# The order of GpSimd's two large multiplies in a selective-scan block on one core

## The chip, the cores and the metric

One core of one Trainium2 chip runs the whole block: layer norm, a selective scan (the Mamba kind) with a gate, a residual, a second layer norm and a top-2 mixture of low-rank experts. The metric is the device time of the core in microseconds (us), as the median of three runs. Two names recur: DVE is VectorE, POOL is GpSimd, and ACT, PE and SP are ScalarE, TensorE and SyncE.

## The reference, cut to what matters

The input is 4 sequences of 2048 tokens with 256 features. The change lies in the scan:

```
u_inner = u @ W_in.T + b_in;  x, z = split(u_inner)          # 512 channels each
dbc = x @ W_x.T + b_x                                        # 16 for delta, 16 for B, 16 for C
delta = softplus(dbc[:16] @ W_dt.T + b_dt);  A = -exp(A_log)  # A: 512 x 16
h = h * exp(delta * A) + (delta * x) * B                     # state, 512 x 16 per token
y = sum over the 16 states of h * C
y = (y + x * D) * silu(z);  out = y @ W_out.T + b_out
```

A feed-forward part with expert routing follows; it is computed by the same engines in between.

## The kernel before, in words

The tokens are worked in 16 chunks of 512. A chunk's scan has 512 channels times 16 states, that is 8192 rows, laid on 128 partitions as 64 units; it is done in 16 **steps** of 4 units each. Step `s` has `m = s // 4` (a block of 128 channels) and `k = s % 4` (four of the states). I write scan(s,j) for unit j of step s, and number the steps of the next chunk from 0 again, with a prime where it matters. For each step:

- POOL does the **B multiply**, B(s): one instruction on 128 x 2048 elements, `hs[s % 4] = dx_rep[m % 2] * b_rep[k]` (`times_b`, line 1051). It waits for the sum of step s-4, whose `hs` buffer it takes over, and at k = 0 for the DMA that brings `dx_rep` (line 446). It signals `input_ready`.
- ACT computes the decay factors `exp(dt * A)` into PSUM, 4 instructions (line 785).
- DVE runs four scans, 128 x 512 each (line 964). scan(s,0) waits for `input_ready` of step s. Each starts from `state`, the last column of the same unit in the chunk before, and the scan of the last chunk is kept by ACT, two units at a time (`keep_state`, line 799).
- The **C product** multiplies the scanned states by C. DVE does units 0 and 1 (line 954), right after scan(s,2). Units 2 and 3 are POOL's in the steps with s % 3 != 0, ten of sixteen (line 1063, `times_c`, which I write C(s)), and DVE's in the other six, after scan(s+1,0). POOL's C(s) waits for all four scans of step s (`scan_done`) and for ACT's copy of their last columns (`state_kept`), because it writes over `hs`. It signals `prod_pool`.
- PE sums over the states into `y_ps` with four matmuls (line 651), two steps behind the scan.

Each engine runs its own program in order, and between the steps stand side jobs, placed by hand in tables (`PE_SIDE`, `ACT_SIDE`, `DVE_SIDE`, `POOL_SIDE`): projections of the next chunk ("pre"), the gate ("main"), output projection and routing of the last one ("post"), the experts ("late"). ACT copies the last columns of units 2 and 3 of step s-1 in its own step s, behind two decay instructions of step s and the side jobs placed at its units 0 and 1.

POOL's step s is B(s+1), then C(s-1) where that one is POOL's, then the side jobs of that row of `POOL_SIDE`. The side jobs are: step 0: A1; 1: O1; 2: S3, G2, G3; 3: V1; 4: U1; 5: A2; 6: S0; 7: O2, G0; 9: S1; 10: G1, S2; 11: V0; 12: U0; 13: W0. S and G (lines 1004 and 1008) are 128 x 512, V and U (lines 1041 and 1001) 128 x 1024, and the others are chains of tiny instructions. R is a job of the last chunk alone. G waits for a Y job of DVE (line 865), the reading of `y_ps`. U produces `z_dt`, which SP stores to DRAM and loads back, spread over the partitions, as `dx_rep`: U0 for the next chunk's m = 0, so that B(0') waits for that way round, and U1 for m = 2, used by B(8).

SP's queue loads `b_rep` and `c_rep` for the next chunk: `b_rep[k]` waits for `input_ready` of the steps 12 + k, `c_rep[k]` for the products of the same steps, POOL's among them. POOL issues no DMA.

Of the kernel before, what the change touches and what calls it, by code (L numbers as in the profile page):

```python
# [36 lines left out]
STEPS = M * KG  # L37
# [202 lines left out]
def block_program(nc, u, w_in, b_in, w_x, b_x, w_dt, b_dt, a_log, d_skip, w_out, b_out, w_ga, b_g, w_i, w_o,  # L240
                  lora_b, ident_in, nsum_in, tri_in, out):
    with ExitStack() as ctx:
# [168 lines left out]
        def side(engine, s, j, parts):  # L411

            for job in SIDE[engine][s][j]:
                if job.split()[1] in parts:
                    yield job[0], int(job[1]), job.split()[1], job
# [577 lines left out]
        def _(pool):  # L993
# [49 lines left out]
            def times_b(c, par, s):  # L1043

                m, k = divmod(s, KG)
                if k == 0:
                    pool.wait_ge(rep_loaded[m % 2], 256 * c + 128 * (m // 2 + 1))
                if m == 0:
                    pool.wait_ge(b_loaded[k], 64 * (c + 1))
                at_least(pool, nsum_done, STEPS * c + s - 3)  # L1050
                nc.gpsimd.tensor_tensor(hs[s % 4][:], dx_rep[m % 2][:], b_rep[:, k, :].unsqueeze(1).to_broadcast([P, J, T]),  # L1051
                                        ALU.mult).then_inc(input_ready, 1)

            def times_c(c, s):

                if s not in POOL_STEPS:
                    return
                k = s % KG
                pool.wait_ge(scan_done, UNITS * c + J * (s + 1))
                pool.wait_ge(state_kept, 2 * (STEPS * c + s + 1))  # L1060
                if s < KG:
                    pool.wait_ge(c_loaded[k], 64 * (c + 1))
                nc.gpsimd.tensor_tensor(hs[s % 4][:, 2:4, :], hs[s % 4][:, 2:4, :],  # L1063
                                        c_rep[:, k, :].unsqueeze(1).to_broadcast([P, 2, T]), ALU.mult).then_inc(prod_pool, 1)

            def body(c, par, parts):
                for s in range(STEPS):
                    if "main" in parts:
                        if s + 1 < STEPS:
                            times_b(c, par, s + 1)  # L1070
                        elif "pre" in parts:
                            times_b(c + 1, par, 0)
                        if s >= 1:
                            times_c(c, s - 1)
                    if s == 0 and "post" in parts:
                        times_c(c - 1, STEPS - 1)
                    for job in side("pool", s, 0, parts):
                        job_pool(*job, c, par)
                if "main" not in parts and "pre" in parts:
                    times_b(0, par, 0)  # L1080

            sweep(pool, body)


# [53 lines left out]
```

## Time and profile before

| | |
|---|---|
| median of 3 runs | 2150.73 us (2149.88 to 2154.53) |
| the profiled execution: its own time | 2150.39 us |
| its span | 2148.6 us |
| POOL busy | 1885.0 us (88%) x892 |
| DVE busy | 1861.7 us (87%) x2256 |
| PE busy | 1693.7 us (79%) x7648 |
| ACT busy | 1422.8 us (66%) x2756 |

The times are read so: the span runs from the first to the last instruction, and the time of a run has some 2 us around it. Busy shares are averages over the start, sixteen chunks and a tail of some 115 us in which the last chunk's experts are computed. What matters for the steps is a chunk in the middle, so the rows further below are taken from there. "POOL hs L1051" is the B multiply, "POOL hs L1063" POOL's C product, "DVE decay L964" a scan. A start-to-start distance is a little shorter than the duration printed, since an engine starts an instruction while the one before writes its last results.

### The profile page before, as it was taken

What the parts mean: (1) busy time and instruction counts of PE and PEld (TensorE: products, weight loads), DVE (VectorE), ACT (ScalarE), POOL (GpSimd) and SP (SyncE); (2) the same over time, 40 slices, a digit from 0 to 9 for tenths busy, and PEclk for the clock granted to TensorE, in tenths of its full rate; (3) what the DMA queues carried; (4) which work ended last, traced back from release to release, by engine and by line L of the source; (5) the groups of instructions that cost most, each with busy time, mean ns of one, the idle gap of its engine ahead of it and who ended that gap; (6) DMA issues with size and microseconds to landing.
All of it is one profiled execution on the core that took longest, in us unless ns stands there. A gap on an engine that the chain in (4) does not pass through costs nothing.

```text
span 2148.6 us, 28539 instructions
## 1 busy us (share of the span) xinstructions
PE 1693.7 (79%) x7648; PEld 939.9 (44%) x7648; DVE 1861.7 (87%) x2256; ACT 1422.8 (66%) x2756; POOL 1885.0 (88%) x892
## 2 busy tenths in 40 slices
PE   3253669888887978888797978879798888877898
PEld 1011225444544545454454544444454445444474
DVE  1698989999998989999898998999899999989810
ACT  2565657767676766777676776867677676766522
POOL 1799999999999999999998998999999998999701
PEclk8575879999998999999999999999999999999998
DMA  3645443553545355354644444454535535453100
GB/s 137 142 106 142 109 118 91 129 128 85 133 102 152 82 128 130 88 120 105 160 98 119 111 104 126 100 145 105 133 91 129 127 83 126 102 150 86 35 8 13
DMA packets 145762, 235.19 MB, mean 109 GB/s; under 512 B 21040, under 2 KB 45872, under 8 KB 145072
## 3 DMA queue, kind: packets, MB, share of 16 engines
q1 hardware_dynamic: 145584, 233.18, 43.4%
q8 instruction: 67, 1.10, 0.2%
q14 instruction: 111, 0.91, 0.1%
HBM read 190.11 MB, written 42.99 MB: 108 GB/s over the span
## 4 chain that ended last, share of the span: by engine, by line
PE 29%; POOL 27%; issue 18%; DVE 10%; DMA 8%; SPq 4%; ACT 3%; POOLq 0%; DVEq 0%; ACTq 0%
POOL hs L1051 14%; POOL hs L1063 6%; PE bank L586 6%; PE y_ps L651 4%; DVE decay L964 4%; PE bank L632 4%; PE bank L600 4%; PE bank L637 4%; PE bank L619 4%; DMA b_rep<-bc_scratch 4%; DVE hs L954 3%; DMA rep_scratch<-z_dt 2%; SPq L446 2%; POOL e_dt L1041 2%; DVE hs L964 2%
## 5 line engine op out<-in xcount | busy, mean ns | idle before, releaser
L1051 POOL TENSOR_TENSOR hs<-dx_rep,b_rep 128x2048 f32<-128x2048 f32 x256 | 1161.7, 4539 | 101.0 <-DMA dx_rep<-rep_scratch 100.4
L964 DVE TENSOR_TENSOR_SCAN decay<-decay,state,hs 128x512 f32<-128x512 f32 x704 | 881.0, 1275 | 98.1 <-POOL hs L1051 86.4
L785 ACT ACTIVATE decay<-dt_rep,a_sb 128x512 f32<-128x512 f32 x1024 | 677.4, 684 | 28.0 <-DMA dx_rep<-rep_scratch 10.7
L651 PE MATMUL y_ps<-hs,nsum 128*32 128x512 f32 x2048 | 298.4, 658 | 207.2 <-POOL hs L1063 96.4
L954 DVE TENSOR_TENSOR hs<-decay,c_rep 128x1024 f32<-128x1024 f32 x352 | 422.9, 1201 | 0.0
L964 DVE TENSOR_TENSOR_SCAN hs<-decay,state,hs 128x512 f32<-128x512 f32 x320 | 406.0, 1269 | 2.2 <-ACT decay L785 1.6
L1063 POOL TENSOR_TENSOR hs<-hs,c_rep 128x1024 f32<-128x1024 f32 x160 | 378.3, 2364 | 4.3 <-ACT state L799 3.7
L632 PE MATMUL bank<-ident,r 128*128 128x128 f32 x1920 | 284.4, 309 | 69.8 <-ACT r L763 30.8
L632 PEld LDWEIGHTS bank<-ident,r 128*128 128x128 f32 x1920 | 260.9, 218 | 135.6 <-ACT r L763 35.1
L619 PE MATMUL bank<-w_i_sb,x_t 128*128 128x512 f32 x512 | 259.9, 631 | 56.9 <-ACT e_dt L706 15.8
L799 ACT COPY state<-decay 128x2 f32<-128x2 f32 x352 | 56.6, 161 | 334.3 <-DVE hs L954 323.2
L586 PE MATMUL bank<-xn_t,w_in_sb 128*128 128x512 f32 x512 | 253.4, 625 | 23.3 <-ACT r L763 15.1
L637 PE MATMUL bank<-w_o_sb,r_t 128*128 128x256 f32 x1024 | 238.8, 387 | 2.2 <-ACT e_gate L725 1.6
L637 PEld LDWEIGHTS bank<-w_o_sb,r_t 128*128 128x128 f32 x1024 | 192.1, 192 | 44.5 <-issue 16.6
L651 PEld LDWEIGHTS y_ps<-hs,nsum 128*32 128x32 f32 x2048 | 43.1, 111 | 317.2 <-issue 220.1
L619 PEld LDWEIGHTS bank<-w_i_sb,x_t 128*128 128x128 f32 x512 | 90.9, 194 | 169.4 <-issue 89.2
L586 PEld LDWEIGHTS bank<-xn_t,w_in_sb 128*128 128x128 f32 x512 | 93.1, 199 | 139.8 <-issue 98.7
L759 ACT ACTIVATE r<-bank,wgt 128x512 f32<-128x512 f32 x128 | 86.4, 675 | 76.5 <-PE bank L620 63.8
L600 PE MATMUL bank<-w_out_sb,gated 128*128 128x256 f32 x512 | 121.8, 382 | 1.7 <-DVE x L873 1.2
L600 PEld LDWEIGHTS bank<-w_out_sb,gated 128*128 128x128 f32 x512 | 94.7, 190 | 34.2 <-DVE x L873 13.9
L770 ACT COPY r_t<-bank 128x512 f32<-128x512 f32 x128 | 73.4, 573 | 42.2 <-PE bank L637 31.7
L763 ACT ACTIVATE r<-bank,wgt 128x512 f32<-128x512 f32 x128 | 86.2, 674 | 19.3 <-PE bank L562 18.4
(99 smaller groups left out, 1731.8 us busy)
## 6 DMA issues: line engine op xcount, KB each, us to landing
dt_rep<-rep_scratch SPq DMA_DIRECT2D x256, 256.0 KB, 4.4
dx_rep<-rep_scratch SPq DMA_DIRECT2D x256, 256.0 KB, 7.3
b_rep<-bc_scratch SPq DMA_DIRECT2D x256, 64.0 KB, 2.9
rep_scratch<-e_dt SPq DMA_DIRECT2D x32, 512.0 KB, 2.8
rep_scratch<-z_dt SPq DMA_DIRECT2D x32, 512.0 KB, 3.7
c_rep<-bc_scratch SPq DMA_DIRECT2D x256, 64.0 KB, 2.1
xin<-in_u SPq DMA_DIRECT2D x16, 512.0 KB, 3.6
xr<-in_u SPq DMA_DIRECT2D x16, 512.0 KB, 3.8
```

Of the source, the lines that this page charges most:

```text
L586: mm = pe.matmul(ps[:], w_in_sb[:, k, col:col + P], xn_t[odd][:, k, :], start=k == 0, stop=k == KD - 1)
L600: pe.matmul(ps[:, 0:D], gated[odd][:, k, i * P:(i + 1) * P], w_out_sb[:, k, :], start=k == 0, stop=False)
L619: pe.matmul(ps[:], x2_t[odd][:, k, t * P:(t + 1) * P], w_i_sb[:, k, cols], start=k == 0, stop=False)
L632: mm = pe.matmul(ps[:, f * P:(f + 1) * P], r[i % 2][:, f * P:(f + 1) * P], ident[:], start=r is r1, stop=r is r2)
L637: mm = pe.matmul(ps[:, 0:D], r_t[:, f, :], w_o_sb[:, f, :], start=f == 0, stop=f == NF - 1)
L651: mm = pe.matmul(y_ps[32 * j:32 * j + 32, :], nsum[:], hs[s % 4][:, j, :], start=k == 0, stop=k == KG - 1)
L759: nc.scalar.activation(r1[i % 2][:], ps[:], ACT.Relu, scale=wgt[odd][:, 0, i // 2:i // 2 + 1]).then_inc(r1_ready, 1)
L785: nc.scalar.activation(decay[:, j, :], dt_rep[m % 2][:, j, :], ACT.Exp, scale=a_sb[:, J * s + j:J * s + j + 1]).then_inc(decay_ready, 1)
L954: v.tensor_tensor(hs[s % 4][:, js, :], decay[:, js, :], c_rep[:, k, :].unsqueeze(1).to_broadcast([P, 2, T]), ALU.mult).then_inc(prod_vecto ...
L964: v.tensor_tensor_scan(hs[s % 4][:, j, :] if kept else decay[:, j, :], decay[:, j, :], hs[s % 4][:, j, :], state[:, b, n:n + 1], ALU.mult, ...
L1051: nc.gpsimd.tensor_tensor(hs[s % 4][:], dx_rep[m % 2][:], b_rep[:, k, :].unsqueeze(1).to_broadcast([P, J, T]), ALU.mult).then_inc(input_re ...
L1063: nc.gpsimd.tensor_tensor(hs[s % 4][:, 2:4, :], hs[s % 4][:, 2:4, :], c_rep[:, k, :].unsqueeze(1).to_broadcast([P, 2, T]), ALU.mult).then_ ...
```

## The change

In GpSimd's program the order inside a step becomes C(s-1), B(s+1), side jobs. The jobs, their waits and their number stay. The product of step 15, which stands at step 0 of the next chunk, moves with the others in the text; since 15 % 3 = 0 it is not POOL's and is no instruction.

```diff
             def body(c, par, parts):
                 for s in range(STEPS):
+                    if s == 0 and "post" in parts:
+                        times_c(c - 1, STEPS - 1)
                     if "main" in parts:
+                        if s >= 1:
+                            times_c(c, s - 1)
                         if s + 1 < STEPS:
                             times_b(c, par, s + 1)
                         elif "pre" in parts:
                             times_b(c + 1, par, 0)
-                        if s >= 1:
-                            times_c(c, s - 1)
-                    if s == 0 and "post" in parts:
-                        times_c(c - 1, STEPS - 1)
                     for job in side("pool", s, 0, parts):
                         job_pool(*job, c, par)
```

## Rows read from the trace of the kernel before

**Rows 1.** Busy us of PE, PEld, DVE, ACT, POOL: first chunk, one in the middle

```profile
67.30:182.10 114.80, 51.22 (x164) 15.16 (x164) 105.40 (x100) 70.86 (x136) 109.27 (x42) 0.65 0.51 120
1044.98:1168.20 123.22, 103.20 (x485) 58.52 (x484) 115.84 (x141) 88.43 (x173) 117.21 (x55) 0.97 0.47 116
```

**Rows 2.** Groups of POOL's instructions by shape: busy, mean ns, idle before

```profile
L1051 POOL TENSOR_TENSOR hs<-dx_rep,b_rep 128x2048 f32<-128x2048 f32 x256 | 1161.7, 4539 | 101.0 <-DMA dx_rep<-rep_scratch 100.4 <-PE y_ps L651 0.5
L1063 POOL TENSOR_TENSOR hs<-hs,c_rep 128x1024 f32<-128x1024 f32 x160 | 378.3, 2364 | 4.3 <-ACT state L799 3.7 <-issue 0.5
L1004 POOL TENSOR_TENSOR z_gate<-z_gate,e_gate 128x512 f32<-128x512 f32 x64 | 82.0, 1282 | 0.0
```

**Rows 3.** POOL in order of time, from step 13 to step 0 of the next chunk

```profile
1028.65 4.55 POOL L1051 TENSOR_TENSOR hs<-dx_rep,b_rep 128x2048 f32<-128x2048 f32 x1
...
1033.31 4.53 POOL L1051 TENSOR_TENSOR hs<-dx_rep,b_rep 128x2048 f32<-128x2048 f32 x1
1037.79 2.37 POOL L1063 TENSOR_TENSOR hs<-hs,c_rep 128x1024 f32<-128x1024 f32 x1
1044.98 4.52 POOL L1051 TENSOR_TENSOR hs<-dx_rep,b_rep 128x2048 f32<-128x2048 f32 x1 [4.83 <-DMA dx_rep<-rep_scratch]
1049.45 2.35 POOL L1063 TENSOR_TENSOR hs<-hs,c_rep 128x1024 f32<-128x1024 f32 x1
1051.76 4.54 POOL L1051 TENSOR_TENSOR hs<-dx_rep,b_rep 128x2048 f32<-128x2048 f32 x1
```

**Rows 4.** What DVE waited for over the whole span: us, times, longest

```profile
DVE decay L964 <- POOL hs L1051: 86.4, 47, 25.2
DVE gated L865 <- PE y_ps L651: 41.8, 30, 3.5
```

**Rows 5.** DVE in order of time: scan(0,0)

```profile
1049.62 1.29 DVE L964 TENSOR_TENSOR_SCAN decay<-decay,state,hs 128x512 f32<-128x512 f32 x1 [3.18 <-POOL hs L1051]
```

**Rows 6.** DVE busy in steps 0 and 1, 4 and 5, 7, 10, 13

```profile
1049.62:1065.66 16.04, 15.65 (x21) 0.89 0.75 180
1078.37:1096.36 17.99, 17.17 (x26) 1.00 0.30 96
1102.20:1109.83 7.63, 7.63 (x9) 1.00 0.19 38
1123.32:1131.56 8.24, 8.24 (x8) 1.00 0.81 170
1147.42:1157.24 9.82, 7.82 (x8) 0.83 0.29 107
```

**Rows 7.** DVE in order of time: scan(s,3) of steps 1, 5, 7, 10, 13

```profile
1064.47 1.28 DVE L964 TENSOR_TENSOR_SCAN hs<-decay,state,hs 128x512 f32<-128x512 f32 x1
...
1093.67 1.25 DVE L964 TENSOR_TENSOR_SCAN hs<-decay,state,hs 128x512 f32<-128x512 f32 x1
...
1108.64 1.27 DVE L964 TENSOR_TENSOR_SCAN hs<-decay,state,hs 128x512 f32<-128x512 f32 x1
...
1130.37 1.27 DVE L964 TENSOR_TENSOR_SCAN hs<-decay,state,hs 128x512 f32<-128x512 f32 x1
...
1156.05 1.27 DVE L964 TENSOR_TENSOR_SCAN hs<-decay,state,hs 128x512 f32<-128x512 f32 x1
```

**Rows 8.** ACT in order of time: the copies of those steps' last columns

```profile
1066.02 0.18 ACT L799 COPY state<-hs 128x2 f32<-128x2 f32 x1
...
1096.68 0.17 ACT L799 COPY state<-hs 128x2 f32<-128x2 f32 x1
...
1112.12 0.19 ACT L799 COPY state<-hs 128x2 f32<-128x2 f32 x1
...
1132.87 0.18 ACT L799 COPY state<-hs 128x2 f32<-128x2 f32 x1
...
1158.64 0.20 ACT L799 COPY state<-hs 128x2 f32<-128x2 f32 x1
```

**Rows 9.** SP's queue in order of time: the last reload of b_rep

```profile
1051.15 1.69 SPq L453 DMA_DIRECT2D b_rep<-bc_scratch  x4
```

## The prediction

> **What bounds the kernel now.** I read the busy time of single chunks first. A chunk in the middle takes 123.22 us, and in it POOL is busy 117.21 us and DVE 115.84 us [rows 1]: two engines are full, and neither has as much as 8 us to spare. The groups of POOL's instructions show what the rest is: before B multiplies POOL idles 101.0 us in the whole run, nearly all for the DMA that brings dx_rep, and before its C products only 4.3 us [rows 2]. POOL in order of time shows the place: once a chunk, before B(0), it stands 4.83 us [rows 3]. DVE's waits are small too: 86.4 us for B multiplies, 25.2 us of it once, at the start, and 41.8 us for the sum that its Y jobs read [rows 4]. So POOL sets the pace, DVE runs just behind it, and what keeps both full is slack between them: POOL can multiply B(s+1) while DVE is still in step s-1, and asks for scan(s-1,3) only after it.
>
> **The change.** No instruction is added or removed. C(s-1), which needs DVE to have finished step s-1, now stands ahead of B(s+1), which DVE needs for step s+1. B(s+1) so gets DVE's progress as a condition that it did not have. Behind a waiting C(s-1) are queued B(s+1), on which DVE waits, and the side jobs of the step. After scan(s-1,3) POOL needs a C and a B, 6.8 us, before DVE may start step s+1, and DVE has only its step s to do meanwhile. Where step s is shorter than that, DVE stalls; where POOL is early, it stalls; and what one loses is no longer made up by the other.
>
> **The terms.** Start to start a B takes 1037.79 - 1033.31 = 4.48 us and a C 1051.76 - 1049.45 = 2.31 us [rows 3]; V and U have the C's shape, 2.31 us. A 128x512 side job prints 1.28 us [rows 2], less the 0.05 us by which 4.54 and 4.48 differ: 1.23 us. From the end of a B to the scan that it releases is 1049.62 - (1044.98 + 4.52) = 0.12 us [rows 3, 5]; I take 0.12 us for the release of a C by ACT's copy too. DVE's stretches run from the start of scan(s,0), which is where each window of [rows 6] begins, to the end of scan(s,3) [rows 7]: steps 0 and 1, 1065.75 - 1049.62 less 0.39 us idle (16.04 - 15.65) = 15.74 us; steps 4 and 5, 1094.92 - 1078.37 = 16.55 us; step 7, 7.71 us; step 10, 8.32 us; step 13, 9.90 us less the 2.00 us that Y2 idles (9.82 - 7.82), which go, since C(11) comes a B multiply sooner: 7.90 us. From scan(s,3)'s end to the end of ACT's copy [rows 7, 8]: step 1, 0.45 us; 5, 1.93; 7, 2.40; 10, 1.41; 13, 1.52. These lags are mostly side jobs that ACT's program puts ahead of the copy (two behind step 7, one long one behind step 10, two behind step 13), so they stay. Behind step 5 the program puts none, and there I take step 1's 0.45 us and keep 1.93 for the range.
>
> **One chunk of the new kernel**, from the end of B(0) to the end of the next chunk's B(0), following whoever is waited for:
> 1. DVE, steps 0 and 1, while POOL does B(1), A1, B(2), O1 (under 11 us) and then waits for C(1)'s data: 0.12 + 15.74 + 0.45 + 0.12 = 16.43 us.
> 2. POOL: C(1), B(3), S3, G2, G3, C(2), B(4): 2 x 6.79 + 3 x 1.23 = 17.27 us. DVE waits for B(3) and B(4).
> 3. DVE, steps 4 and 5: 0.12 + 16.55 + 0.45 + 0.12 = 17.24 us, against POOL's V1, B(5), U1, C(4), B(6), A2 (16.4 us).
> 4. POOL: C(5), B(7): 6.79 us.
> 5. DVE, step 7: 0.12 + 7.71 + 2.40 + 0.12 = 10.35 us, against POOL's S0, B(8), O2, G0 (8.3 us).
> 6. POOL: C(7), B(9), C(8), B(10): 13.58 us. DVE waits for both B.
> 7. DVE, step 10: 0.12 + 8.32 + 1.41 + 0.12 = 9.97 us, against POOL's 8.2 us.
> 8. POOL: C(10), B(12), V0, C(11), B(13): 2 x 6.79 + 2.31 = 15.89 us.
> 9. DVE, step 13: 0.12 + 7.90 + 1.52 + 0.12 = 9.66 us, against POOL's 7 us.
> 10. POOL: C(13), B(15), C(14), B(0): 13.58 us.
>
> The sum is 130.76 us, 7.54 us more than 123.22. POOL waits about 5.6, 0.8, 2.0, 1.8 and 2.7 us in parts 1, 3, 5, 7 and 9, some 13 us in place of its 5.2 at the DMA. That DMA no longer shows: before, B(0) starts 1044.98 - 1028.65 = 16.33 us after U0 [rows 3], now part 9's rest (7.35), 6.79 and 2.31 lie between, 16.4 us. It is just behind the new wait, and takes over if that shrinks.
>
> **What costs nothing.** PE gets POOL's product one B sooner and its sums earlier; they are off the pace. SP: the reload of c_rep comes sooner; that of b_rep waits for B multiplies that come up to 2.31 us later in their step, yet the last one leaves 1051.15 - 1049.50 = 1.65 us after B(0) ends [rows 3, 9], and B(3), which needs it, now starts 18.7 us after. It is hidden by part 1; without that cover it would cost up to its lateness of 2.31 us a chunk. POOL issues no DMA that could be held up. A1 at step 0 may wait for DVE's statistics by a microsecond; part 1's wait covers it.
>
> **Whole run.** The first chunk has fewer side jobs (114.80 us [rows 1]) and the last drains differently, but the alternation of C, B and scans is the same, so I count 16 chunks: 16 x 7.54 = 120.6 us. The sum stands against the profiled execution, 2150.39 us, which is within 0.4 us of the median: 2271 us. Bounds: with every lag at 0.45 us parts 5, 7 and 9 give back 3.98 us, but the DMA claims the wait for C(13) back, 1.0 us, so +4.5 a chunk, 2223 us. With 1.93 us behind step 5, the idle 0.39 us and Y2's 2.00 us kept, it is +11.4 a chunk, 2333 us; these do not all add, and I end the forecast's own range at 2310.
>
> **Rivals.**
> - *Milder, still slower.* If engines slide so that POOL waits only where the trace of before already has POOL early, the price is read off where it is: step 1's copy ends at 1066.20 [rows 8], and POOL, from 1051.76 [rows 3] with two B and the tiny A1 and O1, is free for C(1) at about 1062.4, 3.8 us; step 13's copy ends at 1158.84, and POOL reaches step 14 at 1033.31 + 123.22 = 1156.53, 2.3 us; C(5) and C(7), less early, I estimate at 1.2 us together. That is 7.3 us, less the 4.8 us of DMA wait filled. +2.5 x 16 = 40 us, 2190 us. Against it: it leaves out that DVE is pushed back by 2.31 us wherever it was already waiting.
> - *Faster.* While POOL stands for dx_rep from 1040.15 to 1044.98, C(14) could run there, and now does: its place is ahead of B(0). B(0) is set by U0 and the DMA, and behind it POOL is 2.31 us further. 16 x 2.31 = 37 us, 2113 us. It decides if all waits for scans together stay under 2.31 us a chunk. The Trainium skill says as much (DMA: Bandwidth & Descriptors, Rules for kernel authors): issue the DMA early, compute, and wait on its semaphore late. The trace agrees that such a wait is there. Against this rival is that DVE has no room to be early: it is busy 115.84 of 123.22 us, and in part 1 alone it is some 5 us short.
> - *No change.* Filled wait and new waits cancel: under 0.27 us a chunk. A measurement here can tell 0.2%, 4.3 us.
>
> **Chances.** The forecast 0.70, milder 0.14, faster 0.09, no change 0.04, and 0.03 that it is worse than 2310. The range 2190 to 2310 takes in the forecast's own (2223 to 2310) and the milder case's value. Faster 0.09, same 0.04, slower 0.87.
>
> **What would show it.** Busy times of POOL and DVE a chunk stay within a microsecond, the chunk grows to about 131 us. Idle before POOL's C product goes from 4.3 us to over 150 us, released by ACT's copy; idle before B for dx_rep falls from 100 us to under 35 (the start's 15.8 remains); DVE's wait for B grows from 86 to over 200 us, in scan(4,0), (9,0), (15,0) above all; DVE's wait for y_ps shrinks. C(1) waits longest. The forecast is wrong if POOL's waits before C stay under 5 us a chunk, or if a wait on PE or ACT's decay takes over.

## The result and the profile after

The changed kernel takes 2323.07 us (median of 4 runs, 2320.59 to 2324.80) against 2152.51 us of the kernel before in the same comparison: ratio 1.080, 95% interval 1.078 to 1.082. It is slower by about 170 us, where 120 us were forecast, and lies outside the range. The profiled execution took 2322.81 us.

The first view is the page's busy time and the groups of POOL and DVE that answer to [rows 2, 4], then a chunk in the middle (columns as in [rows 1]).

```profile
PE 1764.6 (76%) x7648; PEld 997.4 (43%) x7648; DVE 1863.5 (80%) x2256; ACT 1426.1 (61%) x2756; POOL 1887.3 (81%) x892
...
L1051 POOL TENSOR_TENSOR hs<-dx_rep,b_rep 128x2048 f32<-128x2048 f32 x256 | 1160.6, 4537 | 18.4 <-DMA dx_rep<-rep_scratch 18.4
L964 DVE TENSOR_TENSOR_SCAN decay<-decay,state,hs 128x512 f32<-128x512 f32 x704 | 881.8, 1276 | 252.2 <-POOL hs L1051 251.1
...
L1063 POOL TENSOR_TENSOR hs<-hs,c_rep 128x1024 f32<-128x1024 f32 x160 | 377.8, 2362 | 239.7 <-ACT state L799 225.7
```

```profile
994.96:1128.92 133.96, 106.87 (x486) 61.04 (x484) 115.81 (x141) 88.75 (x172) 117.30 (x56) 0.94 0.43 107
```

POOL and DVE do the same work in the same time: 117.30 and 115.81 us a chunk against 117.21 and 115.84. Only the chunk is longer, 133.96 against 123.22 us. Sixteen times these 10.74 us are 172 us, as much as the profiled executions differ by, but not each chunk loses the same: from one U0 to the next the loss is 8.1 and 7.5 us in the first two of fifteen distances and 9.5 to 12.0 us in the other thirteen, 11.1 us on average. POOL no longer waits for the DMA (18.4 us, 15.4 of it at the start) but 239.7 us before its C products, and DVE waits 251.1 us for B multiplies in place of 86.4.

POOL in order of time, from one B(0) to the next, shows where. The rows kept are the five C products with a wait and the B multiplies at the ends (x2 joins B(0) and B(1)).

```profile
994.96 9.05 POOL L1051 TENSOR_TENSOR hs<-dx_rep,b_rep 128x2048 f32<-128x2048 f32 x2
...
1015.77 2.37 POOL L1063 TENSOR_TENSOR hs<-hs,c_rep 128x1024 f32<-128x1024 f32 x1 [4.66 <-ACT state L799]
...
1028.60 4.53 POOL L1051 TENSOR_TENSOR hs<-dx_rep,b_rep 128x2048 f32<-128x2048 f32 x1
...
1052.55 2.36 POOL L1063 TENSOR_TENSOR hs<-hs,c_rep 128x1024 f32<-128x1024 f32 x1 [3.08 <-ACT state L799]
...
1069.37 2.37 POOL L1063 TENSOR_TENSOR hs<-hs,c_rep 128x1024 f32<-128x1024 f32 x1 [1.76 <-ACT state L799]
...
1092.94 2.36 POOL L1063 TENSOR_TENSOR hs<-hs,c_rep 128x1024 f32<-128x1024 f32 x1 [1.73 <-ACT state L799]
...
1104.36 4.54 POOL L1051 TENSOR_TENSOR hs<-dx_rep,b_rep 128x2048 f32<-128x2048 f32 x1
...
1119.80 2.36 POOL L1063 TENSOR_TENSOR hs<-hs,c_rep 128x1024 f32<-128x1024 f32 x1 [3.93 <-ACT state L799]
...
1128.92 9.06 POOL L1051 TENSOR_TENSOR hs<-dx_rep,b_rep 128x2048 f32<-128x2048 f32 x2
```

The five waits stand before C(1), C(5), C(7), C(10) and C(13), the places that the prediction names. With B(0) done at 994.96 + 4.53, B(4) at 1033.13, B(13) at 1108.90 and the starts of the C products, and the ends of B(7) and B(10) at 1059.41 and 1083.01, each part of the forecast can be set beside the trace:

| part | forecast us | measured us |
|---|---|---|
| 1: DVE steps 0, 1, then C(1) | 16.43 | 16.28 |
| 2: C(1) to B(4) on POOL | 17.27 | 17.36 |
| 3: DVE steps 4, 5, then C(5) | 17.24 | 19.42 |
| 4: C(5), B(7) | 6.79 | 6.86 |
| 5: DVE step 7, then C(7) | 10.35 | 9.96 |
| 6: C(7) to B(10) | 13.58 | 13.64 |
| 7: DVE step 10, then C(10) | 9.97 | 9.93 |
| 8: C(10) to B(13) | 15.89 | 15.96 |
| 9: DVE step 13, then C(13) | 9.66 | 10.90 |
| 10: C(13) to B(0) | 13.58 | 13.65 |
| sum | 130.76 | 133.96 |

Eight of ten parts hold within 0.4 us. Parts 3 and 9 are short by 2.18 and 1.24 us, together 3.42 us, and the forecast of the other eight is 0.22 us too high in sum. The table is of one chunk; the others of the steady stretch take 134 to 135.6 us.

**Part 3** is a chain through four engines. First DVE's scan(4,0) and PE, then PE's granted clock, then scan(5,3) on DVE, B2 and the copy on ACT:

```profile
1033.24 1.29 DVE L964 TENSOR_TENSOR_SCAN decay<-decay,state,hs 128x512 f32<-128x512 f32 x1 [4.21 <-POOL hs L1051]
...
1037.21 3.58 PE L600 MATMUL bank<-w_out_sb,gated 128*128 128x256 f32 x8 [4.11 <-DVE x L873]
...
1040.74 1.89 PE L600 MATMUL bank<-w_out_sb,gated 128*128 128x256 f32 x8
...
1046.54 3.70 PE L586 MATMUL bank<-xn_t,w_in_sb 128*128 128x512 f32 x8
```

```profile
1037.21:1040.74 3.53, 3.52 (x9) 2.87 (x10) 3.53 (x5) 1.51 (x4) 3.53 (x2) 0.54 0.00 0
1040.74:1044.31 3.57, 3.57 (x16) 2.41 (x14) 3.57 (x5) 2.60 (x5) 3.57 (x2) 1.00 0.33 120
```

```profile
1048.40 1.25 DVE L964 TENSOR_TENSOR_SCAN hs<-decay,state,hs 128x512 f32<-128x512 f32 x1
...
1050.28 0.69 ACT L693 ACTIVATE x_t<-bank,b_in_sb 128x512 f32<-128x512 f32 x1 [1.03 <-PE bank L586]
...
1052.29 0.17 ACT L799 COPY state<-hs 128x2 f32<-128x2 f32 x1
```

DVE stands 4.21 us for B(4). Its additions to the output projection (F, line 873) come late, so PE stands 4.11 us for a bank, and then does eight matmuls of the output projection in 3.58 us; the same eight take 1.89 us a moment later. The granted clock is 0.54 in the first stretch and 1.00 in the second (third number from the right): near the lower of its two levels, 1.2 GHz, after PE had stood, then the upper, 2.4 GHz. PE so reaches B2 late, ACT waits for it, and the copy of step 5's columns, which ACT's program has behind B2, ends at 1052.46, 2.81 us behind scan(5,3) (1049.65). The forecast took 0.45 us. How B2 came to be later than in the kernel before can be read off too, from the same matmuls and B2 there, where scan(4,0) starts at 1078.37:

```profile
1083.19 1.99 PE L600 MATMUL bank<-w_out_sb,gated 128*128 128x256 f32 x8
...
1094.67 0.69 ACT L693 ACTIVATE x_t<-bank,b_in_sb 128x512 f32<-128x512 f32 x1 [1.03 <-PE bank L586]
```

Counted from the start of scan(4,0), PE starts the eight matmuls at 3.97 us, against 4.82 us before the change, and ACT starts B2 at 17.04 us, against 16.30. These 0.74 us are the 1.59 us that the matmuls take longer at the lower clock, less the 0.85 us by which they start earlier.

**Part 9** holds a wait that the forecast sent away:

```profile
1102.05 2.35 POOL L1063 TENSOR_TENSOR hs<-hs,c_rep 128x1024 f32<-128x1024 f32 x1
...
1108.33 0.73 PE L612 MATMUL bank<-ident,pk 128*128 128x128 f32 x4 [2.01 <-DVE pk L933]
...
1109.71 3.19 PE L632 MATMUL bank<-ident,r 128*128 128x128 f32 x16
1112.83 1.07 PE L651 MATMUL y_ps<-hs,nsum 128*32 128x512 f32 x8
1113.97 0.75 DVE L865 SCALAR_TENSOR_TENSOR gated<-x_t,d_sb,y_ps 128x512 f32<-128x512 f32 x1 [1.29 <-PE y_ps L651]
```

C(11) is done at 1104.40, and the sum that Y2 reads starts at 1112.83. It stands in PE's program behind the transposes of `pk`, which wait for DVE's routing chain, and those jobs set its time, not POOL. The trace of before has the same order, so the forecast could have read it there:

```profile
1147.24 2.37 POOL L1063 TENSOR_TENSOR hs<-hs,c_rep 128x1024 f32<-128x1024 f32 x1
1147.42 0.63 PE L612 MATMUL bank<-ident,pk 128*128 128x128 f32 x4 [2.27 <-DVE pk L933]
...
1151.94 1.07 PE L651 MATMUL y_ps<-hs,nsum 128*32 128x512 f32 x8
```

C(11) was done at 1149.61, 2.3 us before the sum that Y2 waited for. PE's stretch from the first transpose to the sum, in the kernel before and in the changed one:

```profile
1147.42:1151.94 4.52, 4.52 (x21) 3.80 (x21) 3.66 (x4) 2.20 (x6) 4.52 (x3) 0.62 0.00 0
1108.33:1112.83 4.50, 4.50 (x21) 3.67 (x21) 3.67 (x4) 1.76 (x5) 4.50 (x3) 0.62 0.14 53
```

Both times PE had stood 2 us or more, and the granted clock is 0.62; its block of sixteen matmuls (line 632) takes 3.19 us, and 2.05 us when it comes again at 1118.10 at clock 1.00. The 0.71 us by which Y2 waits less are about the 0.75 us that DVE now stands for B(13) ahead of it.

### The profile page after: what moved, and what is told of

It is laid out like the page before. It is cut to its first block, busy times and chain, and to the rows that moved or that the text cites. A ratio compares the mean times of both kernels' runs of the same rounds, so it can differ in the third digit from the quotient of the medians.

```text
span 2321.0 us, 28539 instructions
## 1 busy us (share of the span) xinstructions
PE 1764.6 (76%) x7648; PEld 997.4 (43%) x7648; DVE 1863.5 (80%) x2256; ACT 1426.1 (61%) x2756; POOL 1887.3 (81%) x892
## 4 chain that ended last, share of the span: by engine, by line
POOL 32%; DVE 22%; issue 21%; PE 14%; DMA 4%; ACT 3%; SPq 2%; DVEq 1%; POOLq 0%; ACTq 0%
POOL hs L1051 20%; DVE hs L954 8%; POOL hs L1063 7%; DVE decay L964 7%; DVE hs L964 4%; PE bank L632 3%; PE bank L600 3%; PE bank L619 2%; DVE st L835 2%; DMA b_rep<-bc_scratch 2%; PE bank L637 1%; POOL gated L1008 1%; PE bank L586 1%; ACT decay L785 1%; SPq L446 1%
## 5 line engine op out<-in xcount | busy, mean ns | idle before, releaser
L1051 POOL TENSOR_TENSOR hs<-dx_rep,b_rep 128x2048 f32<-128x2048 f32 x256 | 1160.6, 4537 | 18.4 <-DMA dx_rep<-rep_scratch 18.4
L964 DVE TENSOR_TENSOR_SCAN decay<-decay,state,hs 128x512 f32<-128x512 f32 x704 | 881.8, 1276 | 252.2 <-POOL hs L1051 251.1
L1063 POOL TENSOR_TENSOR hs<-hs,c_rep 128x1024 f32<-128x1024 f32 x160 | 377.8, 2362 | 239.7 <-ACT state L799 225.7
L632 PE MATMUL bank<-ident,r 128*128 128x128 f32 x1920 | 314.8, 331 | 126.2 <-ACT x_t L743 54.7
L651 PE MATMUL y_ps<-hs,nsum 128*32 128x512 f32 x2048 | 287.7, 636 | 135.1 <-DVE gated L865 59.8
L632 PEld LDWEIGHTS bank<-ident,r 128*128 128x128 f32 x1920 | 288.5, 238 | 186.7 <-ACT x_t L743 58.3
L619 PE MATMUL bank<-w_i_sb,x_t 128*128 128x512 f32 x512 | 272.1, 657 | 41.3 <-DVE x L876 19.3
L600 PE MATMUL bank<-w_out_sb,gated 128*128 128x256 f32 x512 | 157.5, 463 | 66.6 <-DVE x L873 59.7
L619 PEld LDWEIGHTS bank<-w_i_sb,x_t 128*128 128x128 f32 x512 | 99.0, 211 | 157.6 <-issue 102.3
L600 PEld LDWEIGHTS bank<-w_out_sb,gated 128*128 128x128 f32 x512 | 116.5, 237 | 113.5 <-DVE x L873 73.3
L759 ACT ACTIVATE r<-bank,wgt 128x512 f32<-128x512 f32 x128 | 86.3, 674 | 77.3 <-PE bank L620 68.6
L693 ACT ACTIVATE x_t<-bank,b_in_sb 128x512 f32<-128x512 f32 x64 | 43.9, 686 | 93.9 <-PE bank L586 92.6
```

The source lines that it names most:

```text
L600: pe.matmul(ps[:, 0:D], gated[odd][:, k, i * P:(i + 1) * P], w_out_sb[:, k, :], start=k == 0, stop=False)
L619: pe.matmul(ps[:], x2_t[odd][:, k, t * P:(t + 1) * P], w_i_sb[:, k, cols], start=k == 0, stop=False)
L632: mm = pe.matmul(ps[:, f * P:(f + 1) * P], r[i % 2][:, f * P:(f + 1) * P], ident[:], start=r is r1, stop=r is r2)
L651: mm = pe.matmul(y_ps[32 * j:32 * j + 32, :], nsum[:], hs[s % 4][:, j, :], start=k == 0, stop=k == KG - 1)
L759: nc.scalar.activation(r1[i % 2][:], ps[:], ACT.Relu, scale=wgt[odd][:, 0, i // 2:i // 2 + 1]).then_inc(r1_ready, 1)
L964: v.tensor_tensor_scan(hs[s % 4][:, j, :] if kept else decay[:, j, :], decay[:, j, :], hs[s % 4][:, j, :], state[:, b, n:n + 1], ALU.mult, ...
```

## The experiments

The theory after the result: the loss is the wait that now stands ahead of B, a handshake in which POOL needs DVE's step s-1 and ACT's copy before it may give DVE its step s+1. Rival: any B that comes 2.31 us later in its step starves DVE, whatever stands before it. Kernels e1 to e3, e7 and e8 start from the changed kernel, e4 to e6, e9 and e10 from the one before. Ratios are against the kernel before, run beside each.

### The product that waits for nothing

```diff
-                pool.wait_ge(scan_done, UNITS * c + J * (s + 1))
-                pool.wait_ge(state_kept, 2 * (STEPS * c + s + 1))
...
-                nc.gpsimd.tensor_tensor(hs[s % 4][:, 2:4, :], hs[s % 4][:, 2:4, :], ...
+                at_least(pool, prod_pool, pool_products(c, s) - 1)
+                nc.gpsimd.tensor_tensor(spare[:], row, row, ALU.mult).then_inc(prod_pool, 1)
```

`row` is c_rep broadcast, `spare` a bf16 tile. PE's sum now waits for scan(s,3) as well, and B(s+4) for ACT's copy of step s.

> The changed order, but POOL's C product reads only c_rep and writes a spare tile, so it waits neither for the scans nor for ACT's copy; its time on POOL stays. Left out: the C factor on units 2 and 3 of the ten steps. Theory (the cost is the wait for scan(s-1,3) and ACT's copy that now stands in front of B): the loss goes as a whole, and B(0) is again set by the DMA with 2.31 us of POOL's work moved into its wait, about 121 us a chunk, 2110 us (2095 to 2135). Rival (the cost is that B itself comes 2.31 us later in its step and DVE starves, whatever C waits for): it stays above 2200 us. POOL's idle before the C product near 0 in the first case.

Measured: 2101.33 us, ratio 0.976 (0.974 to 0.978). The groups of POOL:

```profile
L1054 POOL TENSOR_TENSOR hs<-dx_rep,b_rep 128x2048 f32<-128x2048 f32 x256 | 1161.0, 4537 | 106.4 <-DMA dx_rep<-rep_scratch 101.4 <-PE y_ps L653 3.2 <-DMA b_rep<-bc_scratch 1.8
L1066 POOL TENSOR_TENSOR spare<-c_rep 128x1024 bf16<-128x1024 f32 x160 | 303.9, 1899 | 0.0
```

Each B still comes behind a C, and the run is not longer than before: no wait before C, and the wait for dx_rep is back at 101.4 us. One flaw: the product takes 1899 ns, not 2362, which frees POOL of 74 us (160 x 0.46). Even if all of them counted, 2101 + 74 = 2175 us is below the rival's 2200, and leaves at most some 24 of the 170 us for the place of B by itself. The rest of the loss is the wait.

### The product that waits for the scans alone

```diff
-                pool.wait_ge(state_kept, 2 * (STEPS * c + s + 1))
...
-                nc.gpsimd.tensor_tensor(hs[s % 4][:, 2:4, :], hs[s % 4][:, 2:4, :], ...
+                nc.gpsimd.tensor_tensor(hs[s % 4][:, 2:4, 0:T - 1], hs[s % 4][:, 2:4, 0:T - 1], ...
```

B(s+4) takes over the wait for the copy, which is long done by then.

> The changed order, but C(s) leaves the last column out and so waits for the scans alone, not for ACT's copy of that column. Left out: the C factor on the last token of each chunk in those units. Theory: the lags of ACT behind the scans (some 8.8 us a chunk in the five waits: 0.45, 2.8, 2.4, 1.4, 1.5) are part of the handshake and go, until another limit takes over: about 127 us a chunk, 2215 us (2195 to 2240). Rival (ACT's copy is only the last to be seen, the scans bind): 2300 us or more.

Measured: 2239.23 us, ratio 1.041 (1.039 to 1.043), with

```profile
L1063 POOL TENSOR_TENSOR hs<-hs,c_rep 128x1022 f32<-128x1022 f32 x160 | 377.6, 2360 | 145.4 <-DVE hs L964 145.2
```

It is within the theory's range, near its upper end. The instruction costs the same and waits 145 us for the scans instead of 240 us for the copy. Of 170 us lost, 84 go with the wait for ACT's copy; the other 87 stay with the wait for the scans alone.

### ACT's lag behind step 5

All three B jobs behind the copy (e3), then B2 alone (e7); the rows are those of `ACT_SIDE` for steps 5 and 6:

```diff
-    " |  |  | B0 pre, B1 pre, B2 pre",
-    " |  |  | J4 late, T3 late, B3 pre, R2 post",
+    " |  |  | ",
+    " |  | B0 pre, B1 pre, B2 pre | J4 late, T3 late, B3 pre, R2 post",
```

> The changed order, with the three ACT jobs B0, B1, B2 moved from the end of its step 5 to step 6 behind the copy that C(5) waits for. Theory (the lag behind scan(5,3), 2.8 us, is these jobs' waiting for PE): C(5) starts up to 2.3 us sooner, the chunk shortens by 1.5 to 2.3 us, 2287 to 2299 us. Rival (PE's late sum and the Y0 read hold step 5, not the copy): under 0.5 us a chunk, 2315 us or more.

Measured: 2365.91 us, ratio 1.100 (1.098 to 1.101), 43 us slower than the changed kernel. The theory fails; the rival's "2315 us or more" covers the number, but not its reason, that the copy does not hold step 5:

```profile
1074.30 2.35 POOL L1063 TENSOR_TENSOR hs<-hs,c_rep 128x1024 f32<-128x1024 f32 x1 [0.48 <-ACT state L799]
...
1075.60 3.37 PE L586 MATMUL bank<-xn_t,w_in_sb 128*128 128x512 f32 x4 [2.73 <-ACT x_t L693]
...
1080.03 0.75 DVE L865 SCALAR_TENSOR_TENSOR gated<-x_t,d_sb,y_ps 128x512 f32<-128x512 f32 x1 [6.04 <-PE y_ps L651]
1080.08 4.55 POOL L1051 TENSOR_TENSOR hs<-dx_rep,b_rep 128x2048 f32<-128x2048 f32 x1 [3.43 <-PE y_ps L651]
```

The wait before C(5) fell from 3.08 to 0.48 us as meant, but PE then waited for the banks that ACT empties late, its sum of step 3 stands behind that, and the sum is waited for by DVE's Y0 (6.04 us) and by B(7), for the hs buffer (3.43 us). So only B2 was moved:

```diff
+    " |  |  | B0 pre, B1 pre",
+    " |  | B2 pre | J4 late, T3 late, B3 pre, R2 post",
```

> The changed order, with the ACT job B2 alone moved behind the copy that C(5) waits for; B0 and B1 stay, so that PE gets their banks back in time. Theory: the lag behind scan(5,3) falls from 2.8 us to about 1.2 us and the chunk by 1.0 to 1.6 us: 2297 to 2307 us. If PE's sums become late for the bank of B2, as with all three moved: 2323 us or more, with a longer wait of Y0 for y_ps.

Measured: 2302.29 us, ratio 1.072 (1.070 to 1.074), as the theory had it: 21 us faster than the changed kernel, or some 16 us by the two ratios, as the two did not run beside each other. scan(5,3) and the copy in a middle chunk, DVE and ACT in order of time:

```profile
1040.22 1.25 DVE L964 TENSOR_TENSOR_SCAN hs<-decay,state,hs 128x512 f32<-128x512 f32 x1
```

```profile
1042.49 0.18 ACT L799 COPY state<-hs 128x2 f32<-128x2 f32 x1
```

The lag is 1042.67 - 1041.47 = 1.20 us, 1.61 less than in the changed kernel, and the run is shorter by 1.0 to 1.3 us a chunk. The mis-sized term of part 3 is shown as a cause to that extent. How much of the lag is PE's clock was not tested by itself.

### Y2 later

```diff
-    "M1 post | Y2 main |  | ",
+    "M1 post |  |  | Y2 main",
```

> The changed order, with DVE's Y2 moved from behind scan(13,1) to behind scan(13,3). Theory: the 1.3 us that Y2 still waits for the sum (which PE reaches late behind its own jobs, not for POOL's product) and Y2's own 0.65 us leave the path to scan(13,3), and C(13) starts 1.9 us sooner: the chunk is shorter by up to 1.9 us, 2292 to 2305 us. Rival (the wait is for POOL's product and moves along): 2323 us.

Measured: 2360.23 us, ratio 1.100 (1.098 to 1.102), 37 us slower than the changed kernel. Again neither expectation, and again a wait moved:

```profile
1131.08 0.72 DVE L865 SCALAR_TENSOR_TENSOR gated<-x_t,d_sb,y_ps 128x512 f32<-128x512 f32 x1
...
1131.85 1.94 PE L651 MATMUL y_ps<-hs,nsum 128*32 128x512 f32 x8 [2.82 <-DVE gated L865]
...
1136.75 0.69 ACT L759 ACTIVATE r<-bank,wgt 128x512 f32<-128x512 f32 x1 [5.26 <-PE bank L620]
1137.80 0.20 ACT L799 COPY state<-hs 128x2 f32<-128x2 f32 x1
1138.08 2.37 POOL L1063 TENSOR_TENSOR hs<-hs,c_rep 128x1024 f32<-128x1024 f32 x1 [7.22 <-ACT state L799]
```

DVE finds its sum ready now. But PE may not start the next block's sum before Y2 has read `y_ps`, an expert product stands behind it, ACT waits for that product, and the copy that C(13) needs stands behind ACT's wait: 7.22 us in place of 3.93. scan(13,3) itself is done at 1131.15. What Y2's wait costs by itself was not measured by this; that it isn't POOL's doing is read from part 9's rows.

### Which of the ten products costs

The first of the five kernels with a part of the change has this edit, the others another tuple:

```diff
+                        if s >= 1 and s - 1 in (14,):
+                            times_c(c, s - 1)
                         if s + 1 < STEPS:
                             times_b(c, par, s + 1)
                         elif "pre" in parts:
                             times_b(c + 1, par, 0)
-                        if s >= 1:
+                        if s >= 1 and s - 1 not in (14,):
                             times_c(c, s - 1)
```

> C ahead of B only for C(1), C(5), C(7), C(10), C(13), the five that wait in the changed kernel; the other five stand behind B as before. Theory (each handshake costs where DVE has just finished the step whose product POOL asks for): most of the loss stays, about 131 us a chunk, 2275 us (2250 to 2300). Rival (each B that comes 2.31 us later costs the same, whichever product stands before it): half the loss, 2237 us.

> C ahead of B only for C(2), C(4), C(8), C(11), C(14), the five that wait for nothing in the changed kernel. Theory: little is lost, since POOL finds their data ready or waits a little; 124.6 to 125.3 us a chunk, 2180 us (2160 to 2200). Rival (each B 2.31 us later costs the same): 2237 us. The two runs' losses needn't add up to 170 us: the handshakes share DVE's lateness.

> C ahead of B only for C(1), at step 2. Theory: there POOL is well ahead of DVE (steps 0 and 1 of DVE take 15.7 us, POOL's two B 9 us), so the handshake waits some 3.5 us, and B(3) to B(5) come late to DVE; 126.5 us a chunk, 2204 us (2185 to 2215). Rival (ten products ahead share the 170 us evenly): 2167 us.

> C ahead of B only for C(10), at step 11. Theory: in the kernel before POOL reaches step 11 about a microsecond after ACT's copy of step 10's columns and the next long waits of DVE and POOL lie elsewhere, so that B(12)'s 2.31 us are taken back: within 6 us of the kernel before. Rival (each B 2.31 us later costs DVE what it comes late, some 1.7 us a chunk): 2178 us.

> The old order everywhere but at step 15, where C(14) goes ahead of B(0), into the wait for dx_rep. Theory: its data are there about when POOL is free, so nothing is waited for; POOL is 2.31 us ahead behind B(0), of which DVE, next to bind, lets through about 1.0 us a chunk: 2134 us (2113 to 2145). If POOL alone sets the pace: 2113 us. If DVE takes it all: 2150 us.

| ahead of B | us | ratio (95%) |
|---|---|---|
| C(1), C(5), C(7), C(10), C(13) | 2267.54 | 1.057 (1.055 to 1.058) |
| C(2), C(4), C(8), C(11), C(14) | 2185.29 | 1.019 (1.017 to 1.021) |
| C(1) | 2209.81 | 1.029 (1.027 to 1.032) |
| C(10) | 2149.24 | 1.000 (0.999 to 1.001) |
| C(14) | 2134.48 | 0.992 (0.991 to 0.993) |

All five came as the theory had them. In groups of five the cost is 120 and 38 us, not twice the same; C(1) alone costs 60 us, C(10) alone nothing. The second five hold C(14), which alone gains 16 us, so 38 us may be a larger loss less a gain. POOL's C group of the first three kernels idles far more than the 4.3 us of before, though not in proportion to the loss: the second five idle more than C(1) alone and lose less.

```profile
L1063 POOL TENSOR_TENSOR hs<-hs,c_rep 128x1024 f32<-128x1024 f32 x160 | 378.0, 2363 | 182.2 <-ACT state L799 169.4 <-DVE hs L964 11.6 <-PE y_ps L651 1.2
```

```profile
L1063 POOL TENSOR_TENSOR hs<-hs,c_rep 128x1024 f32<-128x1024 f32 x160 | 378.3, 2365 | 74.7 <-ACT state L799 66.1 <-PE y_ps L651 5.0 <-issue 1.8
```

```profile
L1063 POOL TENSOR_TENSOR hs<-hs,c_rep 128x1024 f32<-128x1024 f32 x160 | 378.5, 2366 | 66.5 <-ACT state L799 50.0 <-DVE hs L964 16.5
```

The last kernel, C(14) alone, is 0.8% faster than the kernel before, and is the one to keep. POOL in order of time around its B(0), and its wait for the DMA:

```profile
1036.40 2.36 POOL L1063 TENSOR_TENSOR hs<-hs,c_rep 128x1024 f32<-128x1024 f32 x1 [2.47 <-ACT state L799]
1038.71 9.08 POOL L1051 TENSOR_TENSOR hs<-dx_rep,b_rep 128x2048 f32<-128x2048 f32 x2
```

```profile
POOL hs L1051 <- DMA dx_rep<-rep_scratch: 49.3, 26, 15.2
```

C(14) fills time in which POOL stood for dx_rep: its wait for that falls from 100.4 to 49.3 us. The product now waits itself, here 2.47 us, because POOL is ahead of DVE. That fits with 16 us in place of the 37 us of the forecast's faster rival; no run tests it by itself.

## Why the prediction was right, and where it was wrong

**Right: sign, mechanism and places.** The handshake was the likeliest case, and e1 shows it: the same order without the wait is faster than the kernel before, and at most some 24 us slower if the shorter product is made good. The five waiting products and DVE's waits are where the ten parts put them, the busy times of POOL and DVE did not move, and dx_rep dropped out as a limit. Counting 16 equal chunks came out (172 of 172 us), in part by luck: the first ones lose less than the chunk of the table, most of the others a little more.

**Wrong: the size, by two terms.** The failed step is part 3's lag of ACT's copy behind scan(5,3): "there I take step 1's 0.45 us and keep 1.93 for the range". It measured 2.81 us, and part 3 is 2.18 us too long by it, 35 us in the run at that rate. The program puts nothing directly ahead of that copy, but an in-order engine is also held by what it did not finish before: B2, at the end of ACT's step 5, waits for PE. The trace of before showed 1.93 us for just that reason, and the delayed DVE made it worse through PE's standing and its lower clock. e7 takes most of the lag away and gets 16 to 21 us back.

The second is part 9: "less the 2.00 us that Y2 idles, which go, since C(11) comes a B multiply sooner". 1.29 us stayed and the part is 1.24 us too long, 20 us in the run. That the wait ends with PE's sum says nothing of what the sum waited for; PE came to it late in its own program, in the kernel before as well, and the part of the wait that did go went because DVE itself was later. With PE late, the sign "DVE's wait for y_ps shrinks" failed: it grew from 41.8 to 46.3 us. That these 20 us are lost by Y2's wait is read from the rows; e8 did not isolate it.

**The range.** With both terms as the trace of before has them, 1.93 us behind step 5 and Y2's 2.00 us, the sum would have been 134.24 us against 133.96, though by some luck: the first was 0.88 us too short and the second 0.71 us too long. The forecast's upper bound of 11.4 us a chunk, 2333 us, would have held the time; the range was cut to 2310 because "these do not all add". They did, nearly: both of the larger ones came, as both hang on the same fact, a PE that runs late in its own order.

**The rivals.** The milder one failed as said: DVE was pushed back too. The faster one had a sound core: the wait for dx_rep can be filled, and in e4 it falls by 51 us and the time by 16. The Trainium skill (DMA: Bandwidth & Descriptors, Rules for kernel authors) has the rule to issue the DMA early, compute, and wait on its semaphore late; e4's trace agrees. Nine of the ten moved products have no such wait ahead of them.

**SP and b_rep**, costed at nothing, stayed so: no wait of POOL for b_rep appears among its waits. PE was put at nothing too, as "off the pace". It did wait less for POOL's product (21.8 us of its sums' idle time in place of 96.4), but it was not off the pace: both failed terms run through it.

## What to carry to other kernels

Where two full engines feed each other, put the instruction that the other one waits for ahead of the one that waits for the other, except where the first is held by something else anyway: there a single product moved into the gap won 0.8%, while all ten moved lost 8%. To price such a handshake, follow who is waited for around one period and add the terms; here that would have given the loss to a few per cent of itself, with each lag taken as the trace of before has it, with all that the engine in between still has to finish, not as its program seems to allow. A side job moved off a path may free nothing, since it can also be what gives back a bank or a buffer that a third engine, in its own order, waits for (e3, e8).

## What was not expected of the hardware

POOL's multiply of 128 x 1024 elements takes 1899 ns when both inputs are the same c_rep row and the output is bf16, against 2362 ns with two f32 tiles and an f32 output. Which of the two differences does it was not tried. And PE at work after 4.11 us of standing had a granted clock of 0.54 for 3.53 us: eight matmuls in 3.58 in place of 1.89 us, which made B2 late. Over the run the mean granted clock fell from 0.925 to 0.882, and PE's busy time rose by 71 us with the same 7648 matmuls.
